# Attention and expert layer on one Trainium2 core: the sums over the keys are turned and divided by VectorE in 32 by 32 blocks instead of by TensorE

## What is computed

```python
c_q, c_kv = x @ W_DQ, x @ W_DKV                    # 32 latent dimensions each
Q = concat([heads(c_q @ W_UQ), rope(heads(c_q @ W_QR))])
K = concat([heads(c_kv @ W_UK), rope(x @ W_KR)])   # the rotary part is shared by the heads
scores = where(causal, clip(Q @ K.T, -80, 80), -inf)
attn = softmax(scores / sqrt(12)) @ heads(c_kv @ W_UV)
x = layernorm(x + attn @ W_O)
top = argmax(x @ gate_w.T + gate_b + expert_bias)
y = relu(x @ w1[top] + b1[top]) @ w2[top] + b2[top]
x = layernorm(x + y)
```

## Time and profile before

| | |
|---|---|
| median of 3 runs | 452.9 us (452.47 to 453.28) |
| the profiled execution | 455.0 us |
| its span, first to last instruction | 453.3 us |
| busy in the span: PE, DVE, ACT, POOL | 419.5, 360.3, 355.5, 149.5 us |
| mean granted TensorE clock | 0.963 of full speed |
| attention, first Exp to last clip | 18.2 to 350.8 us |
| place 16 of the last batch: its Exps end, its clip begins | 302.7, 303.1 us |
| ScalarE's copy of the last half's sums | 352.1 to 352.7 us |
| early tiles from start to start, with a job and without | 2.8, 1.9 us |
| first late tile on TensorE | 391.6 us |
| TensorE's clock at half speed in the run, by stretches of 2 us | about 310.6 to 317.4, 389.1 to 395.9 us |

### The profile page before, as it was taken

One profiled execution on the slowest core, in us unless ns is written; L12 is line 12 of the kernel. 1 busy time (PEld: TensorE's weight loads), 2 busy tenths in 40 slices (PEclk: granted clock), 3 DMA queues, 4 the chain that ended last, 5 costly groups with the idle time before them and its releaser, 6 DMA issues. The chain is left out here.

```text
span 453.3 us, 12389 instructions
## 1 busy us (share of the span) xinstructions
PE 419.5 (93%) x4271; PEld 232.0 (51%) x4271; DVE 360.3 (79%) x821; ACT 355.5 (78%) x566; POOL 149.5 (33%) x163
## 2 busy tenths in 40 slices
PE   8599999999999999999999999997999999599970
PEld 6433434444444445444344444333344898599970
DVE  3458887999998889999987999999688487466760
ACT  2569989899998999989899999996897655366650
POOL 7121000036204013412401332240012576778882
PEclk9969999999999999999999999997999999699995
DMA  3666810639761134545301563555200456466610
GB/s 114 141 186 146 213 40 16 138 77 250 173 144 46 48 88 107 130 111 124 101 2 39 127 152 71 123 143 187 67 13 1 122 155 194 140 188 205 190 48 6
DMA packets 33341, 51.80 MB, mean 114 GB/s; under 512 B 5707, under 2 KB 16497, under 8 KB 33280
## 3 DMA queue, kind: packets, MB, share of 16 engines
q1 hardware_dynamic: 25664, 37.17, 33.2%
q10 hardware_dynamic: 5344, 9.57, 7.4%
q0 software_dynamic: 2272, 4.27, 2.8%
HBM read 20.95 MB, written 5.33 MB: 58 GB/s over the span
## 5 line engine op out<-in xcount | busy, mean ns | idle before, releaser
L997 ACT ACTIVATE prob<-ring 128x1024 f32<-128x1024 f32 x288 | 273.8, 1039 | 29.2 <-PE ring L1175 28.5
L1193 PE MATMUL o_acc<-prob,v_stat 128*32 128x512 f32 (+3 forms) x1536 | 156.3, 502 | 3.3 <-DVE prob L671 2.5
L1175 PE MATMUL ring<-queries,keys 32*128 32x512 f32 (+3 forms) x1536 | 126.9, 386 | 4.9 <-DMA queries<-query_parts 4.1
L1175 PEld LDWEIGHTS ring<-queries,keys 32*128 32x128 f32 x1536 | 70.3, 188 | 76.8 <-issue 45.5
L671 DVE SCALAR_TENSOR_TENSOR prob<-prob,mask_hi 128x1024 f32<-128x1024 f32 (+1 forms) x80 | 81.8, 1023 | 0.0
L657 DVE TENSOR_SCALAR prob<-prob 128x2048 f32<-128x2048 f32 x64 | 77.3, 1219 | 5.5 <-ACT prob L997 5.2
L670 DVE TENSOR_SCALAR prob<-prob 128x1024 f32<-128x1024 f32 (+1 forms) x80 | 64.7, 808 | 14.7 <-ACT prob L997 14.6
L1087 ACT ACTIVATE prob<-ring,b1T 128x128 f32<-128x128 f32 x156 | 44.7, 368 | 32.3 <-PE ring L1295 24.1
L565 POOL DMA_INDIRECT by_expert<-xrow,index x32 | 39.7, 1242 | 78.1 <-DVE index L766 70.9
L1193 PEld LDWEIGHTS o_acc<-prob,v_stat 128*32 128x32 f32 x1536 | 34.1, 109 | 57.7 <-issue 39.8
L555 POOL CAST key_parts<-whole_k 128x512 fp32r<-128x512 f32 x15 | 15.4, 1024 | 103.6 <-ACT whole_k L1019 103.6
(11 more groups left out here) (110 smaller groups left out, 341.9 us busy)
## 6 DMA issues: line engine op xcount, KB each, us to landing
queries<-query_parts SPq DMA_DIRECT2D x62, 256.0 KB, 3.9
v_stat<-in_w ACTq DMA_DIRECT2D x34, 256.0 KB
keys<-key_parts SPq DMA_DIRECT2D x64, 128.0 KB, 2.4
queries<-by_expert SPq DMA_DIRECT2D x39, 66.0 KB, 2.0
xrow<-in_x_rows SPq DMA_DIRECT2D x8, 264.0 KB, 4.5
xT<-in_x_T SPq DMA_DIRECT2D x8, 256.0 KB, 2.8
v_stat<-in_w SPq DMA_DIRECT2D x5, 256.0 KB
out<-prob,queries POOLq DMA_INDIRECT x39, 3.0
```

Of the source, the lines that this page charges most:

```text
L997: act.activation(prob[u % P_SLOTS][:, 2 * half:2 * half + 2, :].rearrange("p h s -> p (h s)"), slot(("score", u, half))[:], ACT.Exp, scale ...
L1175: last = pe.matmul(out[:, j % 2 * QC + off:j % 2 * QC + off + w], keys[hg][r, kt * P:(kt + 1) * P], queries[hg][r, qc, part, QC - w:QC], s ...
L1193: last = pe.matmul(o_acc[j * VW:(j + 1) * VW, QC - w:QC], v_stat[b % 2][:, hg, kt, j, :], prob[u % P_SLOTS][:, j, off:off + w], start=begi ...
```

## The change

1. `turn` and `flip` jobs are gone, with the copy of the flipped rows by ScalarE. VectorE turns ScalarE's copy `o_sb` itself in blocks of 32 by 32 into `flipped` (`turn_sum`, one instruction over 512 columns, right behind the clip of the place where the copy is made: places 7, 20, 25 and, of the next batch, 2). Behind it `normalize` takes all 32 reciprocals of a partition in one instruction and multiplies all 256 numbers in one, into `attn_blocks`. For the second pair it turns `attn_blocks` back in a third instruction, again of 512 columns. That result goes straight to the `out` job. `W_O` has its rows reordered on the host to suit.
2. The jobs are placed anew: a batch's own `project` jobs stand at 10 and 13 (before 3 and 8), the next batch's `latent` at 20 and 25 (18 and 20), `v` at 27 and 30 (24 and 30), `project` at 26 and 31 (25 and 31), and `turnx` of the last half at 11 (10). In the first batch `project` stays at 3 and 8.
3. The last half's chain: its sums are turned and divided at tile 0 (before, `turn` at tile 1 and `flip` at tile 2), and every later step stands one tile earlier: `out` at 2, `turnx` at 5, `gate` at 6, `rank` at 7, the routes at 8 and 9, the padding from 8, the plan at 7 to 9.

```diff
@@ -79,11 +79,11 @@
-OWN_JOBS = {3: ("project", 1, 0), 8: ("project", 1, 1),
-            16: ("turn", 0, 0), 23: ("turn", 0, 1), 26: ("turn", 1, 0), 28: ("flip", 0), 29: ("out", 0),
-            33: ("turnx", 0), 34: ("gate", 0), 35: ("rank", 0)}
-LATE_JOBS = {4: ("turn", 1, 1), 6: ("flip", 1), 7: ("out", 1), 10: ("turnx", 1), 12: ("gate", 1), 14: ("rank", 1)}
-NEXT_JOBS = {18: ("latent", 0), 20: ("latent", 1), 24: ("v", 0), 25: ("project", 0, 0), 30: ("v", 1), 31: ("project", 0, 1)}
+OWN_JOBS = {10: ("project", 1, 0), 13: ("project", 1, 1), 29: ("out", 0), 33: ("turnx", 0), 34: ("gate", 0),
+            35: ("rank", 0)}
+LATE_JOBS = {7: ("out", 1), 11: ("turnx", 1), 12: ("gate", 1), 14: ("rank", 1)}
+NEXT_JOBS = {20: ("latent", 0), 25: ("latent", 1), 26: ("project", 0, 0), 27: ("v", 0), 30: ("v", 1),
+             31: ("project", 0, 1)}
 FIRST_JOBS = [("latent", 0), ("project", 0, 0), ("latent", 1), ("v", 0), ("project", 0, 1)]
 FIRST_STEP_JOBS = {1: ("v", 1), 3: ("project", 1, 0), 8: ("project", 1, 1)}
...
@@ -132,11 +130,11 @@
 TAIL_JOBS = [numbered(LATE_JOBS[n], B - 1) for n in sorted(LATE_JOBS)]
-TAIL_AT = {1: "turn", 2: "flip", 3: "out", 6: "turnx", 7: "gate", 8: "rank"}
-PLAN_AT = (8, 9, 10)
+TAIL_AT = {2: "out", 5: "turnx", 6: "gate", 7: "rank"}
+PLAN_AT = (7, 8, 9)
 EARLY_PLAN_AT = (B - 1) * UB + 16
-ROUTE_AT = {9: (0, 1), 10: (2, 3)}
-PAD_AT = 9
+ROUTE_AT = {8: (0, 1), 9: (2, 3)}
+PAD_AT = 8
 PADS_ACT = 2
 LAST_HALF = B * NQC - 1
@@ -234,9 +232,12 @@
         queries = [sb(f"queries{i}", [P, NQC, 2, QC], F32R) for i in range(NHG)]
         v_stat = [sb(f"v_stat{i}", [P, NHG, NKT, HG, VW]) for i in range(2)]
         prob = [sb(f"prob{i}", [P, HG, QC]) for i in range(P_SLOTS)]
         o_sb = [sb(f"o_sb{i}", [P, QC]) for i in range(2)]
-        rsum = sb("rsum", [P, 2 * QC // P * HG])
-        attn = sb("attn", [P, NKT, D])
+        rsum = sb("rsum", [P, QC // VW, 2])
+        attn_blocks = [sb(f"attn_blocks{i}", [P, QC]) for i in range(NQC)]
         xrow = [sb(f"xrow{i}", [P, QT, ROW]) for i in range(Q)]
         flipped = [sb(f"flipped{i}", [P, QT * P]) for i in range(Q)]
...
@@ -371,6 +372,11 @@
             return sums(u // UB, u // NU % PAIRS, UNITS[u % NU][0])
+        def sum_ended(u):
+            return sums_of(u - LAG) if u >= LAG and last_unit(sums_of(u - LAG)) == u - LAG else None
         def last_unit(k):
@@ -671,24 +677,26 @@
                 dve.scalar_tensor_tensor(out=on, in0=on, scalar=P_LO, in1=mask, op0=ALU.max, op1=ALU.min
                                          ).then_inc(clipped, 1)
+            def turn_sum(k):
+                dve.wait_ge(o_out, k + 1)
+                dve.transpose(flipped[k % NQC][:], o_sb[k % 2][:]).then_inc(o_turned, 1)
             def normalize(k):
                 pair, qc = k // NQC % PAIRS, k % NQC
-                dve.wait_ge(turned, k + 1)
-                o = misc[:].rearrange("p (t h c) -> p t h c", h=HG, c=VW)
-                inverse = rsum[:].rearrange("p (g t h) -> p g t h", g=2, h=HG)
-                for g in range(2):
-                    last = dve.reciprocal(inverse[:, g], o[:, :, :, g * VS + DH])
-                last.then_inc(rsum_ready, 1)
+                o = flipped[qc][:].rearrange("p (n r) -> p n r", r=VW)
+                dve.wait_ge(o_turned, k + 1)
+                dve.reciprocal(rsum[:], o[:, :, DH:2 * VS:VS]).then_inc(rsum_ready, 1)
                 dve.wait_ge(rsum_ready, k + 1)
-                tiles = QC // P
-                for g in range(2):
-                    first_col = (pair * 2 + g) * HG * DH
-                    out = attn[:, qc * tiles:(qc + 1) * tiles, first_col:first_col + HG * DH]
-                    last = dve.tensor_tensor(out.rearrange("p t (h d) -> p t h d", d=DH),
-                                             o[:, :, :, g * VS:g * VS + DH],
-                                             inverse[:, g].unsqueeze(3).to_broadcast([P, tiles, HG, DH]), ALU.mult)
-                last.then_inc(attn_ready, 1)
+                rows = attn_blocks[qc][:].rearrange("p (n r) -> p n r", r=VW)[:, :, pair * 2 * DH:(pair + 1) * 2 * DH]
+                dve.tensor_tensor(rows.rearrange("p n (g d) -> p n g d", d=DH),
+                                  o[:, :, 0:2 * VS].rearrange("p n (g c) -> p n g c", c=VS)[:, :, :, 0:DH],
+                                  rsum[:].unsqueeze(3).to_broadcast([P, QC // VW, 2, DH]), ALU.mult).then_inc(attn_ready, 1)
+                if pair == PAIRS - 1:
+                    dve.wait_ge(attn_ready, k + 1)
+                    dve.transpose(flipped[qc][:], attn_blocks[qc][:]).then_inc(attn_turned, 1)
             def add_x(g):
...
@@ -785,8 +791,6 @@
                     latent_evac(*which)
                 if kind == "project":
                     turn_queries(*which)
-                if kind == "turn":
-                    normalize(*which)
                 if kind == "out":
                     add_x(*which)
                 if kind == "gate":
@@ -860,6 +864,8 @@
                 if job_at(u // UB, u % UB):
                     before_clip(*job_at(u // UB, u % UB))
                 clip(u)
+                if sum_ended(u) is not None:
+                    turn_sum(sum_ended(u))
                 if step_job(u - 1, "project"):
                     lower_of_keys(*step_job(u - 1, "project")[1:])
                     lower_of_queries(*step_job(u - 1, "project")[1:])
@@ -871,6 +877,8 @@
                     dve.tensor_tensor(gate_bias[:, 0, :], gate_bias[:, 0, :], gate_bias[:, 1, :], ALU.add
                                       ).then_inc(bias_ready, 1)
                     dve.wait_ge(bias_ready, 1)
+                if sum_ended(u) is not None:
+                    normalize(sum_ended(u))
                 if step_job(u, "out"):
                     moments(step_job(u, "out")[1])
                 if step_job(u + 2, "turnx"):
@@ -967,6 +975,9 @@
             for c in range(TILES + 2):
                 if c < TILES:
                     residual(c)
+                if c == 0:
+                    turn_sum(sums(B - 1, 1, 1))
+                    normalize(sums(B - 1, 1, 1))
                 if 1 <= c <= TILES:
                     y_sum(c - 1)
                 if c + 1 == EARLY_TILES:
@@ -1022,15 +1033,12 @@
                 act.wait_ge(weighted, last_unit(k) + 1)
                 if k >= 2:
-                    act.wait_ge(turned, k - 1)
+                    act.wait_ge(o_turned, k - 1)
                 act.activation(o_sb[k % 2][:], o_acc[:], ACT.Copy).then_inc(o_out, 1)
             def job(kind, i):
                 if kind == "v":
                     v_evac(i)
-                if kind == "flip":
-                    act.wait_ge(flip_mm, i + 1)
-                    act.activation(flipped[i % Q][:], misc[:], ACT.Copy).then_inc(flip_out, 1)
                 if kind == "turnx":
                     act.wait_ge(turnx_mm, i + 1)
                     act.activation(flipped[i % Q][:], misc[:], ACT.Copy).then_inc(turnx_out, 1)
@@ -1050,8 +1058,8 @@
             for u in range(B * UB):
                 exp(u, 0)
                 exp(u, 1)
-                if u >= LAG and last_unit(sums_of(u - LAG)) == u - LAG:
-                    o_evac(sums_of(u - LAG))
+                if sum_ended(u) is not None:
+                    o_evac(sum_ended(u))
                 if step_job(u, "project"):
                     keys_evac(*step_job(u, "project")[1:])
                 elif job_at(u // UB, u % UB):
@@ -1206,20 +1214,8 @@
                 i = which[0]
                 q = i % Q
                 claim_misc((kind, i))
-                if kind == "turn":
-                    pe.wait_ge(o_out, i + 1)
-                    pe.wait_ge(ident_ready, 2)
-                    for t in range(QC // P):
-                        last = pe.transpose(misc[:, t * P:(t + 1) * P], o_sb[i % 2][:, t * P:(t + 1) * P], ident[:])
-                    last.then_inc(turned, 1)
-                elif kind == "flip":
-                    pe.wait_ge(attn_ready, sums(i // Q, 1, q) + 1)
-                    for t in range(QT):
-                        last = pe.transpose(misc[:, t * P:(t + 1) * P], attn[:, q * QT + t, :], ident[:])
-                    last.then_inc(flip_mm, 1)
-                elif kind == "out":
-                    pe.wait_ge(flip_out, i + 1)
+                if kind == "out":
+                    pe.wait_ge(attn_turned, i + 1)
                     pe.wait_ge(out_w_in, 16)
                     for t in range(QT):
                         last = pe.matmul(misc[:, t * D:(t + 1) * D], flipped[q][:, t * P:(t + 1) * P], w_o[:],
...
@@ -1380,6 +1377,13 @@
     return out
+def output_weights(a):
+    rows = a["L0_attn_W_O"].reshape(PAIRS, 2, HG, DH, D).transpose(2, 0, 1, 3, 4)
+    return np.ascontiguousarray(rows.reshape(HEADS * DH, D))
 def constants():
     p = np.arange(P, dtype=np.float32)
...
```

13 lines of the change are left out of this document (5 added, 8 removed).

## The result

The changed kernel takes 450.25 us in the median of its runs (448.5 to 452.2) against 452.9, a ratio of 0.9939 with a 95% interval of 0.9925 to 0.9952. It is faster by 2.6 us, or 0.6%, where 11.4 us were forecast; the time lies outside the range. The profiled execution took 452.16 us with a span of 450.4 (455.0 and 453.3 before).

A forecast was written before the change was run, and what follows sets the result against it. It took each place of attention to be bound by the slower of TensorE and ScalarE. Attention's 8.9 us and the tail chain's 2.5 gave 11.4 us off 452.9, so 441.5 us, with a range of 437.5 to 448.

The forecast's parts named there:

- What the turns and flips give: Attention: removing turns and flips from TensorE gains 3.0 us in each of batches 1 to 3, 1.9 in batch 0.
- The flip at 6: Attention, place 6: removing this flip and its ScalarE copy of 0.63 us gains 0.5 us a batch.
- the turn at 4: Attention, place 4, a unit of two pieces: removing this turn gains its full 0.59 us of TensorE time.
- my gross sum: Attention: gain from all removed turns and flips over four batches, before losses are taken off, 10.9 us.
- VectorE's pieces: Attention: transpose 0.65 us, reciprocal 0.2, product 0.43; VectorE's work goes from 75.0 to 78.0 us a batch.
- I take off 0.3 us for each of three batches: Attention: VectorE's new lumps at place 7 and places 10 to 14 use up its lag; 0.9 us lost in all.
- the 8.9 us of attention: Attention's net gain: 10.9 us less 0.9 for VectorE's lumps and 1.1 at the early plan.
- The moved jobs counted as nothing: Attention: a job costs TensorE the same in any place, counted as zero; if wrong, about 0.2 us a batch.
- They are about 1 us early: Attention, place 18: queries projected from place 10 land about 1 us before the scores; if late, 0 to 2 us a batch.
- The plan, 1.1 us lost: Last batch, early plan behind place 16: VectorE arrives 1.1 us later, so TensorE's wait of 2.5 us becomes 3.6.
- The chain in the tail: Behind attention: the last half's chain one tile earlier brings late tiles forward 2.5 us, leaving a hole of 2.9 us.
- The shared port: Rival in attention: VectorE's product slowed beside GpSimd, about 0.8 us a batch within its room; 442 to 444 us, no separate chance.

The follow-up runs named there:

- e2: Changed kernel with all jobs back at the places of the kernel before, sums still turned by VectorE, tail as changed: 452.78 us, ratio 0.9997.
- e14: Changed kernel with 7 idle semaphore increments added to ScalarE's list, 689 instructions as in the kernel before: 446.61 us, ratio 0.9906.
- e5: Changed kernel with VectorE's transposes, reciprocal and product cut to one block, waits and places kept, output not computed: 446.66 us, ratio 0.9888.
- e1: The changed kernel unchanged, measured again for a second profile: 450.31 us, ratio 0.993.
- e7: Changed kernel with the second projection of the second pair at place 15 instead of 13: 449.91 us, ratio 0.9934.
- e4: Changed kernel with the tail's chain, plan, routes and pads at their old tiles, last turn still at tile 0: 451.11 us, ratio 0.9954.
- e8: Changed kernel with the whole tail as before, the last sum turned by VectorE at tile 1: 450.76 us, ratio 0.995.
- e13: Changed kernel with 28 idle semaphore increments added to ScalarE's list, 710 instructions in all: 447.66 us, ratio 0.9917.
- e6: Changed kernel with the queries' cast of each projection in a step moved from GpSimd to ScalarE, one place later: 447.78 us, ratio 0.989.
- e15: Kernel before with 21 idle semaphore increments added to ScalarE's list, 710 instructions in all: 452.89 us, ratio 1.0034.
- e3: Changed kernel with only the second pair's two projections back, from places 10 and 13 to 3 and 8: 461.97 us, ratio 1.021.
- e9: Changed kernel with 7 waits on a long-reached semaphore written into ScalarE's list: 450.02 us, ratio 0.994.
- e11: Kernel before with 21 waits on a long-reached semaphore written into ScalarE's list: 452.55 us, ratio 0.9996.

## Why the prediction was wrong

- **What the turns and flips give: right where it can be read alone.** Places 16 to 29 of a full batch hold three turns and a flip, 1.9 us by my count. They take 31.4 us before, 29.5 in e2, where the other jobs keep their places, and 29.3 in e14. The flip at 6 gave its 0.5 too (place 7 takes 2.32 us before, 1.83 after). For the turn at 4 no run shows its 0.6. That e5's attention is 11.0 us shorter than before (10.9 was my gross sum) is luck in part: its full batches are shorter by 1.9 and 2.0 where I had 3.0, and the last by 4.7, where the clock falls at the plan before and not in e5.
- **VectorE's pieces: right.** 77.5 us a batch against 78.0. The reciprocal was too low by 0.15 us.
- **"I take off 0.3 us for each of three batches": the first step that failed.** Of the 8.9 us of attention 4.9 came. VectorE's added work costs a full batch 0.9 and 1.1 us (e1 against e5), not 0.3. I judged VectorE by its busy time against the batch. Its list decides: with the jobs at their old places (e2) four instructions in a row (2.5 us) stand ahead of `whole_q`, which frees a PSUM slot for TensorE; at the new places the jobs of 10 to 14 stand behind one another. TensorE waits 1.0 us at place 15 for `whole_q` and 0.5 at place 11 for the scaled rows in each full batch. Neither wait was among those I priced, though the change adds work ahead of both.
- **The moved jobs counted as nothing: wrong, in the other direction.** With VectorE's turns in place they save 1.0 us in each full batch (e1 against e2), since they stand off `whole_q`'s worst places. At place 15 they would save 0.9 more there (e7), but none of it in the time.
- **"They are about 1 us early": not so.** I had the queries 14.2 us behind the start of place 10. In batch 2 VectorE's lag makes the low parts late, and the last of the first group's queries land about 18.7 us behind it, at 219.1, when TensorE starts the scores of place 19 (219.2). The profile names no wait for them there. Yet places 19 to 22 of a full batch take 0.5 to 0.8 us more in most profiles of the changed kernel than in e14's, with the same lists up to there. That this is the queries is not shown. The 3.2 us that TensorE waits for queries in all (4.1 before) stand at the start of the first batch.
- **The plan, 1.1 us lost: wrong.** TensorE's wait is 2.53 us (2.50 in the earlier trace rows). The last batch is 2.2 us shorter, but about 1.0 of that is the clock, at half for 3.4 us instead of 6.8: it is at half for 6.8 in e4, e8 and e13, with the same work up to there, and their last batches (81.7 to 82.0) are 1.0 to 1.2 us shorter than before.
- **The chain in the tail, "it counts in full, because the early tiles end 4.66 us before the late ones can start": the second step that failed.** The early tiles no longer end first. ScalarE's load of code made its relu 1.3 us later than before, TensorE stood still for 2.15 us, and the clock fell behind that where it had not before; a second wait for ScalarE, 3.59 us, stands ahead of the last early tile. So that tile is turned 45.8 us behind the last Exp (36.7 before), where I had the early tiles 0.7 us sooner. The first stall held the chain up too: GpSimd's last route ends 38.4 us behind the last Exp, 38.2 before. With the old length of ScalarE's list (e14) it ends at 35.6, which is the forecast 2.5 us sooner, but the tail is only 1.2 us shorter than before, for the second wait (2.88 us there) still stands between.
- **The shared port: right in kind, the wrong place.** I looked for the price on VectorE; GpSimd paid most of it, 1.86 us a cast against 0.73 before and 0.91 in e5. The Trainium skill ("SBUF — State Buffer", the two sides of SBUF) says that the loser is blocked for the whole instruction. This trace agrees in kind: the cast at 205.41 takes 4.49 us beside five passes of 0.68 to 1.22 us, and ends 0.5 us behind the last of them. Without the cast (e6) places 3 to 15 of a full batch take 0.6 us less; that a whole batch gains is not shown.

Open is what the second stall, ahead of the last early tile, is made of. TensorE waits 3.59 us there for ScalarE in the changed kernel, and e4, e8 and e15 show that it moves with each edit. Open is also why the clock falls behind the first stall in some executions and not in others with as long a wait (2.15 and 2.27 us in the changed kernel and e1, 2.26 in e8). The tail's sum can't be read from its chain alone.

## What to carry to other kernels

When work goes to an engine with room, write down its list at that place and ask what stands behind the new instructions and who waits for it; the busy share of a batch doesn't show that. Removing instructions shifts where an engine's code is loaded: if a time behind a change doesn't follow from its work, put idle instructions back as a first trial. A stall of 2 us on TensorE can cost three times that through the clock (batch 1 of e3) or nothing more (batch 2), so look at each single long wait and at the clock behind it, not at their sum alone. Before a difference between two profiles is put down to an edit, look whether it lies in a stretch that the edit can reach.

## What the runs showed of the hardware that was not expected

- Code loading can be on the path. ScalarE's relu came 2 us later for it (8.0 against 6.0), and 7 instructions moved it by 1.2. The Trainium skill ("Runtime: NRT & Kernel Launch", instruction fetch mechanics) says that fetching is mostly hidden behind the pace of issue; this trace doesn't agree in a stretch where ScalarE issues many small instructions (2.27 us for an issue that takes 0.40 in e13).
- A wait on a semaphore mostly adds no instruction, for it is folded into the next one (7, 28 and 21 waits added 0, 2 and 4 in e9 to e11); an increment adds one each (28 of 28 in e13).
- A reciprocal of 32 columns takes 0.354 us, nearly as long as a product of 256 columns (0.425).
- GpSimd's cast of 128x512 takes between 0.61 and 4.49 us, by what VectorE does beside it.
- After 2.03 us without TensorE work in the middle of attention (e3, batch 1) the granted clock was at its half level, 1.2 GHz, for about 10 us; behind 2.02 us in batch 2 of the same execution and behind a wait of 1.12 us (e14) it stayed at 2.4 GHz.
